# First stage of a layer stack: low rows, projections, slot logits and gate in another order, with the logits' operands filled to 128 partitions

## The chip, the cores and the metric

The kernel runs on one core of one Trainium2 chip. The metric is the time on the device of one execution, in microseconds (us); less is better. The median of three runs is 1717.63 us (1714.06 to 1718.74).

## The reference

Eight sequences of 512 tokens with 128 features go through eight residual layers, each on the layer-normed stream. The change touches only the first layer, a slot attention with 4 heads of 32 features and 64 slots per head. Cut to what matters:

```python
q, k = rope(x @ Wq), rope(x @ Wk); v = x @ Wv
sk = clip(x @ sk_w1 @ sk_w2 + sk_b2, -32, 32)      # sk_w1: 128 -> 16, sk_w2: 16 -> 256
sv = clip(x @ sv_w1 @ sv_w2 + sv_b2, -32, 32)
wk = exp(sk); zk = cumsum(wk, over tokens)
S = where(mask, q @ k.T, 0)
p = softmax((S @ wk) * scale / zk)                  # over the 64 slots
wv = exp(sv); zv = cumsum(wv, over tokens)
A = where(mask, (p / zv) @ wv.T, 0)
o = rms_norm(A @ v) * gnorm_w
g = x @ Wg
x = x + (o * g * sigmoid(g)) @ Wo
```

All of it is in float32. The seven later layers are not touched.

## The kernel before, in words

The work of the first layer lies in `slot_phase` (L2457), with the operations in the class `SlotAttention` (L1828) and the layer norm in `Norm` (L182). It is a software pipeline written out by hand: the program of each engine is a list in which step `s` works on several sequences at once. `batch(s, lag)` gives the sequence `s - lag` if there is one. Lag 0 is the new sequence (norm, projections, rope), lag 1 the middle one (slot weights, scores, logits), lag 2 the last one (softmax, attention, output), lag 3 the output projection and the residual. There are eight sequences and eleven steps; steps 2 to 7 carry all three main lags. The order on every engine is fixed, and one engine waits for another only through semaphores. PSUM has eight banks; the plan in `Banks` (L92) says in which order the products of a step take each bank, and TensorE (PE) waits before it writes a bank until its earlier reader is through.

The operations that the prediction walks through, with the engine of each:

- `rope` (L1958 to L1964, POOL): four products and two sums for queries and keys of one sequence, once all four `qkv_copy` are done. `sum_two`, `Norm.scale`, `sum_three` follow it in POOL's list.
- `states`, `turn_k`, `turn_q`, `scores` (PE): they need the turned queries and keys. `k_copy` (L2089) and `q_copy` (L2096, ACT) bring the transposed keys and queries to SBUF.
- `Norm.normalise` (L262, ACT), then `Norm.turn` (L269, PE) and `Norm.copy` (L275, ACT) for the new sequence.
- `value_log` (L2065) and `value_inverse` (L2070, ACT): one over the running sums of lag 2. `over_sums` (L2204, DVE) needs them; behind it in DVE's list stand `mask_scores` (L2130), and behind those wait `attend` (L2216, PE) and `slot_logits` (L2144, L2150).
- `low` (L1907, PE) makes 32 low rows from the normed sequence, `low_copy` (L1913, ACT) puts them into the tile `lowT`, whose row 33 is ones; `slot` (L1969, PE) multiplies these 33 rows with `slot_w2` for one quarter of the tokens, `clip` (L1979, DVE) and `weights` (L1983, ACT) finish the slot weights.
- `gate` (L1928, PE), `gate_guard` and the three steps of `gate_sigmoid` (L1935 to L1944, ACT), `gate_product` (L1948, DVE).
- `project` (L1918, PE) and `qkv_copy` (L1923, ACT), four times a sequence; `mean_squares` (L2251), `project_out` (L2275), `inverse_rms` (L2256, L2258), `apply_rms` (L2263), `apply_gate` (L2269), `add` (L2281); `scan` (L2058, DVE), the running sums.

PE's step before ends with `project` 3 and 2, `low`, `gate`, `slot` 1 and 0, and the next begins with `slot` 2 and 3 and `key_sums` 0. ACT's step begins with the rest of the last projection, `low_copy`, the whole gate chain and `weights` 1 and 0. After this phase the stages of the later layers follow one another, each with its own programs.

Of the kernel before, what the change touches and what calls it, by code (L numbers as in the profile page):

```python
# [14 lines left out]
P = 128  # L15
NB = 8
T = 512
# [1810 lines left out]
class SlotAttention:  # L1828
# [5 lines left out]
    def __init__(self, nc, sv, tag, norm, last_slot):  # L1834
# [11 lines left out]
        self.last_slot = last_slot  # L1846
        self.lowT = sb("lowT", [2 * LOW + 1, T])
        self.qkv = sb("qkv", [P, NT, 3 * D], 3)
# [40 lines left out]
    def set_up_rows(self, dve):  # L1889
        for u in range(2):  # L1890
            last = dve.memset(self.lowT[u][2 * LOW:2 * LOW + 1, :], 1.0)
        last.then_inc(self.ones_row, 1)
# [16 lines left out]
    def low_copy(self, act, b):  # L1909
        act.wait_ge(self.low_done, b + 1)  # L1910
        act.wait_ge(self.ones_row, 1)
        wait_ge(act, self.slot_done[self.last_slot], b - 1)
        act.activation(self.lowT[b % 2][0:2 * LOW, :], self.banks.of("low")[0:2 * LOW, :], ACT.Copy).then_inc(self.lowT_ready, 1)  # L1913
# [22 lines left out]

    def gate_sigmoid(self, act, b):
        sig = self.sig[b % 2]
        act.wait_ge(self.g_steps, 3 * b + 1)
        act.activation(sig[:, :], sig[:, :], ACT.Exp, scale=-1.0, bias=self.consts[:, 1:2]).then_inc(self.g_steps, 1)  # L1940
        act.wait_ge(self.g_steps, 3 * b + 2)
        act.activation(sig[:, :], sig[:, :], ACT.Ln, bias=self.sv.ones[:, 0:1]).then_inc(self.g_steps, 1)
        act.wait_ge(self.g_steps, 3 * b + 3)
        act.activation(sig[:, :], sig[:, :], ACT.Exp, scale=-1.0).then_inc(self.sig_ready, 1)  # L1944
# [512 lines left out]
def slot_phase(nc, sv, tag, a):  # L2457
# [3 lines left out]
    with nc.cleanup_on_exit():  # L2461
# [5 lines left out]
        banks = Banks(nc, tag, 8, (  # L2467
            ("slot2", 2, 1, (slot.clip_done[2],)), ("slot3", 3, 1, (slot.clip_done[3],)), ("zk0", 5, 1, (slot.zk_ready[0],)),
            ("state1", 7, 1, (slot.state_ready[1],)), ("kT", 5, 1, (slot.kT_ready,)), ("qT", 6, 1, (slot.qT_ready,)),
# [4 lines left out]
            ("A0", 0, 2, (slot.a_ready[0],)), ("A1", 1, 2, (slot.a_ready[1],)), ("A2", 2, 2, (slot.a_ready[2],)), ("A3", 3, 2, (slot.a_ready[3],)),  # L2474
            ("L1", 6, 1, (slot.lg_ready[1],)), ("L0", 5, 1, (slot.lg_ready[0],)), ("proj1", 1, 0, (slot.qkv_ready[1],)),
            ("o", 4, 2, (slot.on_ready,)), ("proj0", 0, 0, (slot.qkv_ready[0],)), ("wvT1", 6, 1, (slot.wvT_ready[1],)),
            ("ms", 5, 2, (slot.ln_ready,)), ("out", 6, 3, (slot.x_done,)), ("proj3", 3, 0, (slot.qkv_ready[3],)), ("proj2", 2, 0, (slot.qkv_ready[2],)),
            ("low", 4, 0, (slot.lowT_ready,)), ("gT", 5, 0, (slot.gated_ready,)), ("slot1", 1, 0, (slot.clip_done[1],)), ("slot0", 0, 0, (slot.clip_done[0],))))
        norm.banks = slot.banks = banks
# [14 lines left out]
        with nc.Block() as block:  # L2494
# [16 lines left out]
            def _(pe):  # L2511
                pe.wait_ge(constants, ALL_CONSTANTS)
                pe.wait_ge(memsets, 3)
                for s in STEPS:
                    for b in batch(s, 1):
                        slot.slot(pe, b, 2)
                        slot.slot(pe, b, 3)
                        slot.key_sums(pe, b, 0)
                        slot.states(pe, b, 1)
                        slot.turn_k(pe, b)  # L2520
                        slot.turn_q(pe, b)
                        slot.states(pe, b, 2)
                        slot.scores(pe, b)
# [18 lines left out]
                    for b in batch(s, 1):  # L2542
                        slot.slot_logits(pe, b, 1)
                        slot.slot_logits(pe, b, 0)
                    for b in batch(s, 0):
# [5 lines left out]
                    for b in batch(s, 1):  # L2551
                        slot.turn_values(pe, b, 1)
                    if s == LAST:
                        pe.wait_ge(folding.products_kept, 1)
# [7 lines left out]
                    for b in batch(s, 0):  # L2562
                        slot.project(pe, b, 3)
                        slot.project(pe, b, 2)
                        slot.low(pe, b)
                        slot.gate(pe, b)
                        slot.slot(pe, b, 1)
                        slot.slot(pe, b, 0)
                folding.turn_ternary(pe, 0)

            @block.scalar
            def _(act):
# [4 lines left out]
                for s in STEPS:  # L2577
                    for b in batch(s, 1):
                        slot.qkv_copy(act, b, 2)
                        slot.low_copy(act, b)  # L2580
                        slot.gate_guard(act, b)
                        slot.gate_sigmoid(act, b)
                        slot.weights(act, b, 1)
                        slot.weights(act, b, 0)
                    for b in batch(s, 2):
                        slot.exponential(act, b)
                    if s == LAST:
                        folding.copy(act)
                    for b in batch(s, 1):
                        slot.weights(act, b, 2)  # L2590
                        slot.key_log(act, b, 0)
                    for b in batch(s, 2):
                        slot.value_log(act, b)
                    for b in batch(s, 1):
                        slot.k_copy(act, b)
                        slot.q_copy(act, b)
                    for b in batch(s, 0):
                        norm.normalise(act, b)
                    for b in batch(s, 1):
                        slot.weights(act, b, 3)  # L2600
                    for b in batch(s, 2):
                        slot.value_inverse(act, b)
                    for b in batch(s, 1):
                        slot.key_log(act, b, 1)
                        slot.values_copy(act, b, 0)
                        slot.key_inverse(act, b)
                    for b in batch(s, 0):
                        norm.copy(act, b)
                    if s == LAST:
                        folding.keep_products(act)  # L2610
                    for b in batch(s, 2):
                        slot.square(act, b)
                    for b in batch(s, 0):
                        slot.qkv_copy(act, b, 1)
                    for b in batch(s, 1):
                        slot.values_copy(act, b, 1)
                    for b in batch(s, 2):
                        slot.inverse_rms(act, b)
                    for b in batch(s, 0):
                        slot.qkv_copy(act, b, 3)  # L2620
                        slot.qkv_copy(act, b, 0)
                folding.finish_proj(act)

            @block.vector
            def _(dve):
                slot.set_up_rows(dve)
                for s in STEPS:
                    for b in batch(s, 0):
                        norm.statistics(dve, b)
                        norm.aggregate(dve, b)  # L2630
                    if s == 0:
                        dve.wait_ge(constants, ALL_CONSTANTS)
                        dve.wait_ge(memsets, 3)
                    for b in batch(s, 1):
                        slot.clip(dve, b, 1)
                        slot.clip(dve, b, 0)
                        slot.gate_product(dve, b)
                        slot.clip(dve, b, 2)
                    for b in batch(s, 2):
                        slot.scan(dve, b, 1)  # L2640
                    for b in batch(s, 1):
                        slot.clip(dve, b, 3)
                        slot.state_copy(dve, b, 1)
# [3 lines left out]
                    for b in batch(s, 1):  # L2647
                        slot.state_copy(dve, b, 2)
                        slot.mask_scores(dve, b, 0)
                    for b in batch(s, 2):  # L2650
# [24 lines left out]
                    for b in batch(s, 1):  # L2675
                        slot.scale_logits(dve, b, 0)
                        slot.maximum(dve, b)
                        slot.subtract(dve, b)
                        slot.scan(dve, b, 0)
                    for b in batch(s, 2):  # L2680
                        slot.apply_rms(dve, b)
                    if s != LAST:
                        for b in batch(s, 3):
                            slot.add(dve, b)
                    for b in batch(s, 2):
                        slot.apply_gate(dve, b)
                folding.finish_fc(dve)
# [318 lines left out]
def program(nc, a, out):  # L3006
# [35 lines left out]
    sv.slot_w1 = sb("slot_w1", [P, 2 * LOW], F32)  # L3042
    sv.slot_w2 = sb("slot_w2", [2 * LOW + 1, 2 * SH * SM], F32)
    sv.l1b_w = sb("l1b_w", [P, 6, D], F32)
# [31 lines left out]
```

## Time and profile before

| | before |
|---|---|
| median of three runs | 1717.63 us |
| time of the profiled execution | 1717.68 us |
| its span (first to last instruction) | 1715.9 us |
| PE busy | 1520.5 us, 89% of the span |
| DVE busy | 1189.5 us, 69% |
| ACT busy | 1256.8 us, 73% |
| POOL busy | 529.5 us, 31% |
| mean granted TensorE clock | 0.940 of full speed |

A timeline row gives the start in us from the span's start, the time it took, the engine, the line, the operation and its tiles, how many instructions are merged in it, and in brackets how long the engine was idle before it and who ended that. Busy time of PE is modelled at its ends, so the distance from one start to the next is the safer measure.

### The profile page before, as it was taken

The page shows a single profiled execution, that of the slowest core. Times are in us where ns is not written, and L with a number is a line of the kernel's source. Part 1 is how long each engine was busy: PE and PEld are TensorE (multiplying, and loading weights), DVE is VectorE, ACT ScalarE, POOL GpSimd, SP SyncE. Part 2 cuts the span into 40 slices and gives each one's busy share as a digit, 9 for nine tenths or more (in the row PEclk, how much of TensorE's full clock was granted, in tenths as well). Part 3 has the DMA queues.
Part 4 walks back from the last instruction along what each step waited for, and adds up shares of the span by engine and source line. Part 5 has one row for each costly group of instructions (what it writes and reads, how often), then busy time and mean ns, then how long its engine had stood idle before and what let it go on. Part 6 is the DMA issues. An engine that isn't in the chain of part 4 may idle for free. (4 is left out here: it accounts for less than half of the span.)

```text
span 1715.9 us, 37883 instructions
## 1 busy us (share of the span) xinstructions
PE 1520.5 (89%) x14142; PEld 731.0 (43%) x14142; DVE 1189.5 (69%) x1931; ACT 1256.8 (73%) x2113; POOL 529.5 (31%) x908
## 2 busy tenths in 40 slices
PE   7899997784699999998889999968874999999998
PEld 4676665662133333336633333345541333333256
DVE  4677778798999999966710000048878999999743
ACT  4555553597488888885679999925763888888863
POOL 3432342552323333334400000013212233333362
PEclk9899989797699999999989999989986999999999
DMA  4000000025534343320133333201333333333211
GB/s 132 1 1 1 1 1 1 1 78 156 155 97 110 108 112 107 109 64 27 38 94 95 96 100 97 68 24 49 99 106 113 84 90 92 87 93 93 67 38 38
DMA packets 140410, 125.42 MB, mean 73 GB/s; under 512 B 38410, under 2 KB 118340, under 8 KB 140228
## 3 DMA queue, kind: packets, MB, share of 16 engines
q1 hardware_dynamic: 130980, 121.90, 23.9%
q0 software_dynamic: 8192, 0.77, 0.9%
q8 instruction: 113, 1.85, 0.5%
q14 instruction: 69, 0.57, 0.1%
q10 hardware_dynamic: 1056, 0.33, 0.1%
HBM read 77.19 MB, written 44.96 MB: 71 GB/s over the span
## 5 line engine op out<-in xcount | busy, mean ns | idle before, releaser
L1700 ACT ACTIVATE m_probs<-m_psum 128x512 f32<-128x512 f32 (+1 forms) x768 | 511.7, 762 | 63.1 <-PE m_psum L1623 62.2
L1700 ACT ACTIVATE e_probs<-e_psum 128x512 f32<-128x512 f32 x512 | 276.3, 596 | 53.3 <-PE e_psum L1623 51.8
L1740 DVE TENSOR_REDUCE a_minus_max<-m_psum 128x2 f32<-128x1024 f32 x256 | 300.9, 1219 | 14.3 <-PE m_psum L1632 13.0
L1740 DVE TENSOR_REDUCE a_minus_max<-e_psum 128x2 f32<-128x1024 f32 x256 | 300.6, 1219 | 14.4 <-PE e_psum L1632 13.0
L1623 PE MATMUL m_psum<-m_q_stack,m_k_stack 114*32 114x512 bf16 (+1 forms) x4096 | 295.8, 385 | 6.7 <-DMA m_k_stack<-n_parts 4.6
L1643 PE MATMUL m_psum<-m_probs,m_v_ones 128*32 128x512 f32 x2048 | 271.0, 602 | 3.4 <-DVE m_pair L1690 2.1
L1623 PEld LDWEIGHTS m_psum<-m_q_stack,m_k_stack 114*32 114x32 bf16 (+1 forms) x4096 | 106.9, 96 | 225.8 <-issue 126.2
L1623 PE MATMUL e_psum<-e_q_stack,e_k_stack 126*32 126x512 bf16 x2048 | 157.8, 385 | 2.2 <-ACT e_probs L1700 2.2
L1643 PE MATMUL e_psum<-e_probs,e_v_ones 128*32 128x512 f32 x1024 | 132.2, 593 | 0.0
L1632 PE MATMUL m_psum<-m_k_stack,m_q_stack 48*128 48x512 bf16 x512 | 93.0, 400 | 32.0 <-DVE a_minus_max L1740 24.4
L1632 PE MATMUL e_psum<-e_k_stack,e_q_stack 60*128 60x512 bf16 x512 | 93.9, 400 | 27.9 <-DVE a_minus_max L1740 22.6
L1583 POOL CAST a_max_parts<-a_minus_max 128x16 bf16<-128x16 f32 x64 | 12.6, 197 | 324.6 <-DVE a_minus_max L1740 324.6
L1522 POOL DMA_DIRECT2D m_q_stack<-a_max_rows x128 | 76.3, 602 | 58.6 <-DVE a_max_rows L1745 51.4
L1522 POOL DMA_DIRECT2D e_q_stack<-a_max_rows x128 | 76.2, 601 | 58.0 <-DVE a_max_rows L1745 51.0
L1623 PEld LDWEIGHTS e_psum<-e_q_stack,e_k_stack 126*32 126x32 bf16 x2048 | 43.7, 95 | 116.9 <-ACT e_probs L1700 70.5
L1958 POOL TENSOR_TENSOR s_rope_product<-s_qkv,rope 128x512 f32<-128x512 f32 x32 | 40.3, 1291 | 156.0 <-ACT s_qkv L1923 156.0
L1577 POOL COPY m_v_ones<-vtok 128x128 f32<-128x128 f32 x64 | 18.5, 289 | 222.1 <-PE m_psum L1643 222.1
L1643 PEld LDWEIGHTS m_psum<-m_probs,m_v_ones 128*32 128x32 f32 x2048 | 53.0, 110 | 78.5 <-ACT m_probs L1700 51.9
L1690 DVE COPY slot_w<-m_psum 128x512 f32<-128x512 f32 x8 | 5.5, 691 | 113.4 <-PE m_psum L1643 113.4
L1632 PEld LDWEIGHTS m_psum<-m_k_stack,m_q_stack 48*128 48x128 bf16 x512 | 24.6, 93 | 114.6 <-issue 53.7
L1632 PEld LDWEIGHTS e_psum<-e_k_stack,e_q_stack 60*128 60x128 bf16 x512 | 24.6, 93 | 113.2 <-issue 53.8
L1413 DVE RECIPROCAL slot_wo<-slot_wo 128x64 f32<-128x64 f32 x24 | 13.1, 546 | 80.3 <-DMA slot_wo<-a_context_pairs 80.3
(401 smaller groups left out, 2648.1 us busy)
## 6 DMA issues: line engine op xcount, KB each, us to landing
polar_q<-m_late SPq DMA_DIRECT2D x24, 256.0 KB, 3.0
polar_k<-m_late SPq DMA_DIRECT2D x24, 256.0 KB, 3.4
m_q_stack<-polar_q SPq DMA_DIRECT2D x64, 96.0 KB, 2.3
m_k_stack<-polar_k SPq DMA_DIRECT2D x64, 96.0 KB, 2.4
ctx<-a_context_pairs SPq DMA_DIRECT2D x48, 128.0 KB
a_context_pairs<-slot_w SPq DMA_DIRECT2D x24, 256.0 KB, 2.2
m_q_stack<-dist_parts SPq DMA_DIRECT2D x192, 32.0 KB
m_k_stack<-dist_parts SPq DMA_DIRECT2D x192, 32.0 KB
```

The lines of the kernel that those rows point to most:

```text
L1413: dve.reciprocal(self.inverse, self.sums).then_inc(self.inverted, 1)
L1522: pool.dma_start(rows[:, :, j:j + 32], self.max_rows[j:j + 32, :]).then_inc(self.rows_loaded, 16)
L1577: pool.tensor_copy(self.buf.v_ones[n % 2][:, :, :, DH * (n % 2):DH * (n % 2) + DH], self.sv.vtok[:, tiles_of(b), :].rearrange("p t (h d) - ...
L1583: pool.tensor_copy(self.max_parts[:, 0, :], self.minus_max[n % 2][:, :]).then_inc(self.hi_ready, 1)
L1623: last = pe.matmul(self.ps_s[i % self.PAIRS][r:r + 32, j, :], self.buf.k_stack[g][0:self.rows, h, c * P + r:c * P + r + 32], self.buf.q_st ...
L1632: pe.matmul(to[:, :], self.buf.q_stack[g][part, h, t * P:(t + 1) * P], self.buf.k_stack[g][part, h, :], start=True, stop=True).then_inc(se ...
L1643: last = pe.matmul(self.ps_pv[32 * h:32 * h + self.buf.VW, :], self.buf.v_ones[m % 2][:, c, h, :], self.buf.probs[(NT * m + c) % self.buf. ...
L1690: copied = eng.tensor_copy(self.buf.pair[k % 2][:, :], self.ps_pv[:, :])
L1700: act.activation(self.buf.probs[(NT * m + c) % self.buf.PROBS][:, self.WIDE * part:self.WIDE * (part + 1), :], self.ps_s[i % self.PAIRS], ...
L1740: dve.tensor_reduce(self.minus_max[n % 2][:, k:k + NT + 1:NT], self.ps_r[r % self.TWOS], AX.X, ALU.max, negate=True).then_inc(self.two_fre ...
L1958: pool.tensor_tensor(self.products[n][:, :, :, :], halves[:, :, :, i, :], table, ALU.mult).then_inc(self.rope_steps, 1)
```

## The change

`lowT` and `slot_w2` grow from 33 to 128 partitions. The rows beyond 33 are zeros on both sides, so the products stay the same: `slot_w2` is cleared whole as before, and each `lowT` is cleared once at the start. `gate_sigmoid` is split into three calls, so that ACT's list can put other work between them. The orders of the lists are changed: on PE `low` goes between the two halves of `slot_logits`, `project` 3 and 2 ahead of `mean_squares`, `gate` behind `slot` 1 and 0, and `key_sums` 0 between `slot` 2 and `slot` 3. `gT` moves from bank 5 to bank 4. On ACT `weights` 1 and 0 close a step, and the gate chain comes after `key_log` 0, laced with `k_copy`, `q_copy` and `weights` 3; `value_log` and `normalise` come behind it. On DVE the statistics of the next sequence move ahead of `scan` 0, `clip` 1 and 0 and `scan` 1 move to the end of the step, and `gate_product` moves behind `state_copy` 2. POOL's list stays.

```diff
-        self.lowT = sb("lowT", [2 * LOW + 1, T])
+        self.lowT = sb("lowT", [P, T])
...
     def set_up_rows(self, dve):
         for u in range(2):
+            last = dve.memset(self.lowT[u][:, :], 0.0)
+        last.then_inc(self.ones_row, 1)
+        dve.wait_ge(self.ones_row, 1)
+        for u in range(2):
             last = dve.memset(self.lowT[u][2 * LOW:2 * LOW + 1, :], 1.0)
...
-            ("slot2", 2, 1, ...), ("slot3", 3, 1, ...), ("zk0", 5, 1, ...),
+            ("slot2", 2, 1, ...), ("zk0", 5, 1, ...), ("slot3", 3, 1, ...),
...
-            ("low", 4, 0, (slot.lowT_ready,)), ("gT", 5, 0, (slot.gated_ready,)), ("slot1", 1, 0, ...), ("slot0", 0, 0, ...)))
+            ("slot1", 1, 0, ...), ("slot0", 0, 0, ...), ("gT", 4, 0, (slot.gated_ready,))))
...
 PE
                         slot.slot(pe, b, 2)
+                        slot.key_sums(pe, b, 0)
                         slot.slot(pe, b, 3)
-                        slot.key_sums(pe, b, 0)
...
                         slot.slot_logits(pe, b, 1)
+                    for b in batch(s, 0):
+                        slot.low(pe, b)
+                    for b in batch(s, 1):
                         slot.slot_logits(pe, b, 0)
...
                         slot.turn_values(pe, b, 1)
+                    for b in batch(s, 0):
+                        slot.project(pe, b, 3)
+                        slot.project(pe, b, 2)
...
                     for b in batch(s, 0):
-                        slot.project(pe, b, 3)
-                        slot.project(pe, b, 2)
-                        slot.low(pe, b)
-                        slot.gate(pe, b)
                         slot.slot(pe, b, 1)
                         slot.slot(pe, b, 0)
+                        slot.gate(pe, b)
 ACT
                     for b in batch(s, 1):
-                        slot.qkv_copy(act, b, 2)
-                        slot.low_copy(act, b)
-                        slot.gate_guard(act, b)
-                        slot.gate_sigmoid(act, b)
-                        slot.weights(act, b, 1)
-                        slot.weights(act, b, 0)
+                        slot.weights(act, b, 2)
                     for b in batch(s, 2):
                         slot.exponential(act, b)
...
                     for b in batch(s, 1):
-                        slot.weights(act, b, 2)
                         slot.key_log(act, b, 0)
+                        slot.gate_guard(act, b)
+                        slot.k_copy(act, b)
+                        slot.gate_exponential(act, b)
+                        slot.q_copy(act, b)
+                        slot.gate_logarithm(act, b)
+                        slot.weights(act, b, 3)
+                        slot.gate_sigmoid(act, b)
                     for b in batch(s, 2):
                         slot.value_log(act, b)
-                    for b in batch(s, 1):
-                        slot.k_copy(act, b)
-                        slot.q_copy(act, b)
                     for b in batch(s, 0):
                         norm.normalise(act, b)
-                    for b in batch(s, 1):
-                        slot.weights(act, b, 3)
                     for b in batch(s, 2):
                         slot.value_inverse(act, b)
...
                         norm.copy(act, b)
+                        slot.low_copy(act, b)
...
+                        slot.qkv_copy(act, b, 3)
+                        slot.qkv_copy(act, b, 2)
                     for b in batch(s, 2):
                         slot.inverse_rms(act, b)
                     for b in batch(s, 0):
-                        slot.qkv_copy(act, b, 3)
-                        slot.qkv_copy(act, b, 0)
+                        slot.weights(act, b, 1)
+                        slot.weights(act, b, 0)
 DVE
                     for b in batch(s, 1):
-                        slot.clip(dve, b, 1)
-                        slot.clip(dve, b, 0)
-                        slot.gate_product(dve, b)
                         slot.clip(dve, b, 2)
-                    for b in batch(s, 2):
-                        slot.scan(dve, b, 1)
...
                         slot.state_copy(dve, b, 2)
+                        slot.gate_product(dve, b)
                         slot.mask_scores(dve, b, 0)
...
+                    for b in batch(s + 1, 0):
+                        norm.statistics(dve, b)
+                        norm.aggregate(dve, b)
                         slot.scan(dve, b, 0)
                     for b in batch(s, 2):
                         slot.apply_rms(dve, b)
+                    for b in batch(s, 0):
+                        slot.clip(dve, b, 1)
+                        slot.clip(dve, b, 0)
+                    for b in batch(s, 2):
+                        slot.apply_gate(dve, b)
                         ... slot.add(dve, b)
-                        slot.apply_gate(dve, b)
+                    for b in batch(s, 1):
+                        slot.scan(dve, b, 1)
...
-    sv.slot_w2 = sb("slot_w2", [2 * LOW + 1, 2 * SH * SM], F32)
+    sv.slot_w2 = sb("slot_w2", [P, 2 * SH * SM], F32)
```

## Rows read from the trace of the kernel before

**Rows 1.** Timeline of PE: one step at 177 to 211 us, and the first step.

```profile
27.79 0.70 PE L269 MATMUL s_bank<-ident,s_n_xn 128*128 128x128 f32 x4
...
177.88 1.04 PE L1907 MATMUL s_bank<-s_n_xnT,slot_w 128*32 128x512 f32 x2
...
179.91 3.70 PE L1969 MATMUL s_bank<-slot_w,s_lowT 33*128 33x512 f32 x8
...
187.39 0.70 PE L2103 MATMUL s_bank<-vtok,s_qk 128*128 128x256 f32 x2 [0.50 <-POOL s_qk L1964]
...
197.08 2.06 PE L2216 MATMUL s_bank<-s_zvT,s_wvT 64*128 64x128 f32 x32 [0.65 <-DVE ctx L2130]
...
208.14 1.02 PE L2251 MATMUL s_bank<-s_o,s_same_head 128*128 128x512 f32 x2
...
210.05 1.46 PE L1918 MATMUL s_bank<-slot_w,s_n_xnT 128*128 128x384 f32 x4
211.44 1.04 PE L1907 MATMUL s_bank<-s_n_xnT,slot_w 128*32 128x512 f32 x2
```

**Rows 2.** Timeline of POOL: rope's pieces in four of its eight runs.

```profile
21.83 1.26 POOL L1964 TENSOR_TENSOR s_qk<-s_rope_product 128x512 f32<-128x512 f32 x1
...
48.90 1.27 POOL L1964 TENSOR_TENSOR s_qk<-s_rope_product 128x512 f32<-128x512 f32 x1
...
178.83 5.01 POOL L1958 TENSOR_TENSOR s_rope_product<-s_qkv,rope 128x512 f32<-128x512 f32 x4 [21.77 <-ACT s_qkv L1923]
...
185.15 2.19 POOL L1964 TENSOR_TENSOR s_qk<-s_rope_product 128x512 f32<-128x512 f32 x1
...
253.78 2.18 POOL L1964 TENSOR_TENSOR s_qk<-s_rope_product 128x512 f32<-128x512 f32 x1
```

**Rows 3.** Timeline of ACT in the same step.

```profile
180.74 0.72 ACT L1940 ACTIVATE s_sig<-s_sig,s_consts 128x512 f32<-128x512 f32 x1
...
183.82 1.04 ACT L2178 ACTIVATE s_logits<-s_logits 128x1024 f32<-128x1024 f32 x1
...
188.96 0.60 ACT L2089 ACTIVATE s_kT<-s_bank 128x512 f32<-128x512 f32 x1
189.46 0.59 ACT L2096 ACTIVATE s_qT<-s_bank 128x512 f32<-128x512 f32 x1
189.97 1.65 ACT L262 ACTIVATE s_n_xn<-x,s_n_shift,s_n_rstd 128x128 f32<-128x128 f32 x4
191.52 0.61 ACT L1983 ACTIVATE vtok<-vtok 128x512 f32<-128x512 f32 x1
192.04 1.04 ACT L2070 ACTIVATE s_zvT<-s_zvT 128x1024 f32<-128x1024 f32 x1
```

**Rows 4.** Timeline of DVE in the same step, and one row of step 8.

```profile
175.82 1.23 DVE L2058 TENSOR_TENSOR_SCAN s_zvT<-ones,s_wvT 128x512 f32<-128x512 f32 x1 [1.44 <-ACT s_wvT L2051]
...
178.24 0.68 DVE L2269 TENSOR_TENSOR s_og<-s_og,s_sig 128x512 f32<-128x512 f32 x1
...
184.12 2.16 DVE L2058 TENSOR_TENSOR_SCAN s_zvT<-ones,s_wvT 128x512 f32<-128x512 f32 x1
...
193.19 0.69 DVE L2204 TENSOR_TENSOR s_zvT<-s_bank,s_zvT 128x512 f32<-128x512 f32 x1 [0.37 <-ACT s_zvT L2070]
...
261.36 0.68 DVE L2204 TENSOR_TENSOR s_zvT<-s_bank,s_zvT 128x512 f32<-128x512 f32 x1
```

**Rows 5.** Windows: stretch, length, busy PE, PEld, DVE, ACT, POOL, clock, DMA.

```profile
184.00:186.00 2.00, 2.00 (x5) 1.64 (x6) 2.00 (x2) 1.39 (x2) 2.00 (x2) 0.50 0.00 0
...
214.00:216.00 2.00, 2.00 (x6) 0.94 (x5) 1.21 (x2) 1.90 (x4) 2.00 (x2) 1.00 0.00 0
...
218.00:220.00 2.00, 2.00 (x6) 1.04 (x4) 2.00 (x2) 0.94 (x2) 2.00 (x2) 0.51 0.01 4
```

**Rows 6.** Timeline of DVE at the start of the span.

```profile
0.89 1.02 DVE L1891 MEMSET s_lowT<- 1x512 f32 x2 [0.89 <-PEq L3065]
...
4.14 0.87 DVE L213 BATCH_NORM_STATS2 s_n_stats<-x 128x6 f32<-128x128 f32 x4 [2.22 <-DMA x<-n_L_attn_a_hidden_states]
```

More of the change, by code:

```diff
@@ L1910, in low_copy @@
         act.wait_ge(self.low_done, b + 1)
-        act.wait_ge(self.ones_row, 1)
+        act.wait_ge(self.ones_row, 2)
         wait_ge(act, self.slot_done[self.last_slot], b - 1)
@@ L1935, in gate_guard, with gate_exponential @@
         act.activation(sig[:, :], self.banks.of("gT")[:, :], ACT.Relu, bias=self.consts[:, 1:2]).then_inc(self.g_steps, 1)
-    def gate_sigmoid(self, act, b):
+    def gate_exponential(self, act, b):
         sig = self.sig[b % 2]
@@ L1940, in gate_sigmoid, with gate_logarithm @@
         act.activation(sig[:, :], sig[:, :], ACT.Exp, scale=-1.0, bias=self.consts[:, 1:2]).then_inc(self.g_steps, 1)
+    def gate_logarithm(self, act, b):
+        sig = self.sig[b % 2]
         act.wait_ge(self.g_steps, 3 * b + 2)
         act.activation(sig[:, :], sig[:, :], ACT.Ln, bias=self.sv.ones[:, 0:1]).then_inc(self.g_steps, 1)
+    def gate_sigmoid(self, act, b):
+        sig = self.sig[b % 2]
         act.wait_ge(self.g_steps, 3 * b + 3)
@@ L2467, in slot_phase @@
         banks = Banks(nc, tag, 8, (
-            ("slot2", 2, 1, (slot.clip_done[2],)), ("slot3", 3, 1, (slot.clip_done[3],)), ("zk0", 5, 1, (slot.zk_ready[0],)),
+            ("slot2", 2, 1, (slot.clip_done[2],)), ("zk0", 5, 1, (slot.zk_ready[0],)), ("slot3", 3, 1, (slot.clip_done[3],)),
             ("state1", 7, 1, (slot.state_ready[1],)), ("kT", 5, 1, (slot.kT_ready,)), ("qT", 6, 1, (slot.qT_ready,)),
@@ L2474, in slot_phase @@
             ("A0", 0, 2, (slot.a_ready[0],)), ("A1", 1, 2, (slot.a_ready[1],)), ("A2", 2, 2, (slot.a_ready[2],)), ("A3", 3, 2, (slot.a_ready[3],)),
-            ("L1", 6, 1, (slot.lg_ready[1],)), ("L0", 5, 1, (slot.lg_ready[0],)), ("proj1", 1, 0, (slot.qkv_ready[1],)),
+            ("L1", 6, 1, (slot.lg_ready[1],)), ("low", 4, 0, (slot.lowT_ready,)), ("L0", 5, 1, (slot.lg_ready[0],)), ("proj1", 1, 0, (slot.qkv_ready[1],)),
             ("o", 4, 2, (slot.on_ready,)), ("proj0", 0, 0, (slot.qkv_ready[0],)), ("wvT1", 6, 1, (slot.wvT_ready[1],)),
-            ("ms", 5, 2, (slot.ln_ready,)), ("out", 6, 3, (slot.x_done,)), ("proj3", 3, 0, (slot.qkv_ready[3],)), ("proj2", 2, 0, (slot.qkv_ready[2],)),
-            ("low", 4, 0, (slot.lowT_ready,)), ("gT", 5, 0, (slot.gated_ready,)), ("slot1", 1, 0, (slot.clip_done[1],)), ("slot0", 0, 0, (slot.clip_done[0],))))
+            ("proj3", 3, 0, (slot.qkv_ready[3],)), ("proj2", 2, 0, (slot.qkv_ready[2],)), ("ms", 5, 2, (slot.ln_ready,)), ("out", 6, 3, (slot.x_done,)),
+            ("slot1", 1, 0, (slot.clip_done[1],)), ("slot0", 0, 0, (slot.clip_done[0],)), ("gT", 4, 0, (slot.gated_ready,))))
         norm.banks = slot.banks = banks
@@ L2608, in _ @@
                         norm.copy(act, b)
+                        slot.low_copy(act, b)
                     if s == LAST:
                         folding.keep_products(act)
+                    for b in batch(s, 0):
+                        slot.qkv_copy(act, b, 1)
                     for b in batch(s, 2):
@@ L2613, in _ @@
                     for b in batch(s, 0):
-                        slot.qkv_copy(act, b, 1)
+                        slot.qkv_copy(act, b, 0)
                     for b in batch(s, 1):
                         slot.values_copy(act, b, 1)
+                    for b in batch(s, 0):
+                        slot.qkv_copy(act, b, 3)
+                        slot.qkv_copy(act, b, 2)
                     for b in batch(s, 2):
@@ L2626, in _ @@
                 slot.set_up_rows(dve)
+                norm.statistics(dve, 0)
+                norm.aggregate(dve, 0)
+                dve.wait_ge(constants, ALL_CONSTANTS)
+                dve.wait_ge(memsets, 3)
                 for s in STEPS:
[L2628 to L2633, printed above, removed]
                     for b in batch(s, 1):
-                        slot.clip(dve, b, 1)
-                        slot.clip(dve, b, 0)
-                        slot.gate_product(dve, b)
                         slot.clip(dve, b, 2)
-                    for b in batch(s, 2):
-                        slot.scan(dve, b, 1)
-                    for b in batch(s, 1):
                         slot.clip(dve, b, 3)
@@ L2681, in _ @@
                         slot.apply_rms(dve, b)
+                    for b in batch(s, 0):
+                        slot.clip(dve, b, 1)
+                        slot.clip(dve, b, 0)
+                    for b in batch(s, 2):
+                        slot.apply_gate(dve, b)
                     if s != LAST:
@@ L2684, in _ @@
                             slot.add(dve, b)
-                    for b in batch(s, 2):
-                        slot.apply_gate(dve, b)
+                    for b in batch(s, 1):
+                        slot.scan(dve, b, 1)
                 folding.finish_fc(dve)
```

## The prediction

> **What bounds the first stage now.** The page's first part shows PE as the busiest engine, 89% of the span, so at first sight PE bounds it. The timelines of the four engines, read side by side for one step, say otherwise for this stage. Follow one turn of the pipeline. P is the moment at which PE has issued the last `project` (177.88, where `low` begins [rows 1]). The copies and rope's start follow by 178.83, and rope ends at R = 187.34 [rows 2]: P to R is 9.46 us. PE waits for it (0.50 us [rows 1]), turns the keys, and ACT's `k_copy` starts at 188.96, R + 1.62 [rows 3]. ACT goes on to `q_copy`, `normalise`, `weights` 3 and `value_inverse`, and DVE's `over_sums` starts at 193.19, which is 4.23 after `k_copy` [rows 4]. Four more pieces of DVE's list lie ahead of `attend` at 197.08 (3.89 us; PE waits 0.65 [rows 1]). From there PE works without a long wait to the next P at 211.44: 14.36 us [rows 1]. The five legs, 9.46 + 1.62 + 4.23 + 3.89 + 14.36, make 33.56 us, the distance from one P to the next. So the step is a ring of dependences through POOL, ACT, DVE and PE, and an operation is free if it lies beside this ring and paid for in every step if it lies on it.
>
> From the second rope's end (50.17) to the eighth's (255.96) six turns take 205.79 us, 34.30 each [rows 2]. That is 4.4 us more than six times 33.56.
>
> **The clock.** The windows of 2 us show it. In 214 to 216 us PE is busy all 2.00 us, with the 33-row products, at a granted clock of 1.00; in 218 to 220 it is as busy and the clock is 0.51. In the step before, it is 0.50 in 184 to 186 [rows 5], just behind the run of eight 33-row products that begins at 179.91 [rows 1]. Every step has such a fall behind this run. Where it is short it lies inside the wait for rope and the step keeps its 33.56 us; where it is long it reaches past R, and the step takes about 1.5 us more: three of six, by the 4.4 us above.
>
> **The change, part by part.**
>
> *The zero rows.* A product over 33 rows and one over 128 stream the same 512 columns; two of them take 2.03 us together as `low` and `gate` (177.88 to 179.91), four slots 3.70 [rows 1]: no cost, at most 0.1 us a slot. If the clock then stays up, the gain is what the fall costs now, 0 to 1.5 us a step, 4.4 us in all, and no more, because in the other steps rope is waited for anyway. I take it as gained: the full-clock step is my base. The two memsets more (two small ones take 1.02 [rows 6]) fit in the 2.22 us in which DVE waits for the first input; without that cover they would cost about 1 us once.
>
> *PE from `attend` to P.* `low` comes in (half of 2.03, 1.0 us). `mean_squares` and `project_out` go behind P (210.05 - 208.14 = 1.91 us [rows 1]). The leg becomes 14.36 + 1.0 - 1.91 = 13.45. `low` needs `Norm.copy`, which ACT has done long before; `outputs` needs `low_copy` because of bank 4, hidden behind the second `slot_logits` and a projection. Gain 0.91.
>
> *PE from P to R.* It now has `mean_squares`, `project_out`, `slot` 1 and 0, `gate`, `slot` 2, `key_sums` 0 and `slot` 3, some 7.6 us against 9.46: PE waits nearly 2 us for rope instead of 0.5. That costs nothing itself; the ring passes through POOL here. `gate`'s new wait, for `apply_rms` to free bank 4, is met while `slot` 1 and 0 run.
>
> *ACT between `k_copy` and `over_sums`.* This is the costly part. Now four operations stand there. After the change they are, in ACT's order: `k_copy`, the gate's first step, `q_copy`, its second, `weights` 3, its third, `value_log`, `normalise`, `value_inverse`. None from the gate's first step on can start before `k_copy`, which waits for rope. A copy of 0.60 lets the next start after 0.50 (188.96 to 189.46), so I take 0.1 off each duration: 0.50 + 0.62 + 0.50 + 0.62 + 0.52 + 0.52 + 0.94 (as the 1.04 of the 1024-wide exponential) + 1.55 (189.97 to 191.52) + 1.15 (192.04 to `over_sums` at 193.19) [rows 3, 4]. That is 6.92 against 4.23: 2.69 us more. What is late next: `normalise` starts 4.22 us after `k_copy` instead of 1.01 (188.96 to 189.97), so `Norm.turn` on PE, and all that is queued behind it (`states` 3, `key_sums` 1, `turn_values`, `attend`), waits. `gate_product`, which must free bank 4 for `Norm.turn`, is ready before the normed rows are and hides behind them. `over_sums` blocks DVE's list, with three `mask_scores` behind it, so `attend` moves by the full 2.69.
>
> *Port and queue in P to `k_copy`.* `scan` 1 runs beside rope now: it takes 2.16 instead of 1.23, and rope's last piece 2.19 instead of 1.26 [rows 2, 4]. After the change it still does. New beside rope is `apply_gate` (0.68 [rows 4]), which reads two SBUF operands as the scan does. Bounds for what rope loses: 0 and 0.68; by the scan's row, where 0.93 of 1.23 was lost, 0.5, which I take. `clip` 2, `weights` 2, `exponential` and `key_log` 0 queue behind the later `scan` 1 and come through about when rope ends; `k_copy` is 0 to 0.6 late by them, I take 0. The statistics move into time in which DVE waited.
>
> New turn: 9.46 + 0.5 + 1.62 + 6.92 + 3.89 + 13.45 = 35.84, against 34.30 as measured: 1.54 more, six times, 9.2 us.
>
> *The ends.* At the start `low` precedes the projections: rope 0 is 1.0 us later. In step 1, without lag 2, `Norm.turn` began 4.70 after R (27.79 against 23.09 [rows 1, 2]); ACT now starts `normalise` at 1.62 + 3.28 = 4.90 and has all four pieces at 6.5, so `Norm.turn` ends some 1.5 later; less the 0.91, 0.6. In step 8, without lag 0, `over_sums` came at R + 5.40 (261.36 [rows 4] after 255.96 [rows 2]); now 1.62 + 3.28 + 0.94 + 1.15 = 6.99: 1.6. The last two steps keep their chain.
>
> Sum: 9.2 + 1.0 + 0.6 + 1.6 = 12.4 us. The profiled execution took 1717.68 us, as the median (1717.63): **1730 us**. Bounds: with no loss of rope and 0.1 us less for each of seven ACT operations the turn is 34.6 and the sum 5 us; with both losses at their upper ends 36.6 and 17 us: 1723 to 1735.
>
> **The rivals.**
>
> *The clock falls all the same, in the new waits.* For it: PE now waits about 2 us for rope, then again for the normed rows and `over_sums`; against it: the rows above show the fall behind 33-row products on a busy PE. If it falls where the turn goes through PE behind R, it costs the 1.5 us of the long falls now, eight times: 12 us on top, 1742. This is also the case in which zeros do nothing. The Trainium skill (TensorE: Matmul & The Clock Gate, section "Why this matters for your kernels") puts a fall down to idle gaps between bursts of matmuls, and by it zero rows would help nothing while longer waits would hurt; this trace disagrees so far, since PE was busy 2.00 of 2.00 us ahead of the fall.
>
> *Faster: ACT's longer list hides.* It decides at `over_sums`: if that starts under R + 6.8 (5.85 now and the 0.91 gained behind `attend`), the step gets shorter. If ACT had the gate's steps and `value_log` done ahead of R, where it idles, the turn would be 33.56 - 0.91 = 32.65: six times 1.65 gained, 0.9 in step 1, 1.0 lost at the start, 1708. For it: ACT has idle time enough, and the clock's gain comes with it. Against: in the program's order they stand behind `k_copy`, which can't precede rope.
>
> *About even.* If the operations overlap better than I take (34.3 a turn) and only the ends lose, 1720.
>
> **How the numbers follow.** A measurement of this kernel can tell about 0.3%, 5 us, from no change. My forecast 0.53, the falling clock 0.15, about even 0.15, faster 0.17. So slower 0.68, same 0.15, faster 0.17. The likeliest case's own range is 1723 to 1735. The range of 8 in 10 reaches from 1710 into the falling clock at 1744; left out is most of the faster case.
>
> **What would show it.** In the profile after: rope's ends about 35.8 us apart; PE waiting about 2 us for rope at L2103 and 1 to 2 us at L269 for ACT's normed rows; `over_sums` at R + 8.5; the clock at 1.00 behind the slots. Wrong it is if `over_sums` comes before R + 7, if rope starts more than 1 us behind P, or if the clock's falls grow longer than now.

## The result

The changed kernel takes 1735.98 us in the median (1734.28 to 1738.26, four runs) against 1718.14: 1.0107 of before (95% interval 1.0092 to 1.0122), so slower by 1.1%, clear of the noise. The profiled execution took 1735.14 us, with a span of 1733.3; before it was 1717.68 and 1715.9, so the profiles differ by 17.4 us.

The first stage carries nearly all of it. The first row of the next stage on PE, of before and then of after (timelines):

```profile
311.20 1.63 PE L269 MATMUL m_psum<-ident,m_probs 128*128 128x128 f32 x4 [6.42 <-ACT m_probs L262]
```

```profile
327.97 1.63 PE L269 MATMUL m_psum<-ident,m_probs 128*128 128x128 f32 x4 [6.42 <-ACT m_probs L262]
```

That is 16.8 of the 17.4 us. (Line numbers after: rope L1968 to L1974, `states` L2113, `k_copy` L2099, `value_log` L2075, `value_inverse` L2080, `over_sums` L2214, `slot` L1979, `weights` L1993, the gate's ACT lines L1939 to L1954.) One step of after, read as [rows 1 to 4] were, PE first:

```profile
188.54 1.02 PE L2261 MATMUL s_bank<-s_o,s_same_head 128*128 128x512 f32 x2
...
198.33 0.70 PE L2113 MATMUL s_bank<-vtok,s_qk 128*128 128x256 f32 x2 [2.29 <-POOL s_qk L1974]
...
204.78 1.39 PE L269 MATMUL s_bank<-ident,s_n_xn 128*128 128x128 f32 x4 [0.82 <-ACT s_n_xn L262]
...
207.68 1.19 PE L2018 MATMUL s_bank<-vtok,causal 128*128 128x256 f32 x2 [0.67 <-DVE s_zvT L2214]
...
211.66 2.06 PE L2226 MATMUL s_bank<-s_zvT,s_wvT 64*128 64x128 f32 x32
...
224.77 1.02 PE L2261 MATMUL s_bank<-s_o,s_same_head 128*128 128x512 f32 x2
```

ACT and DVE of the same step:

```profile
199.97 0.60 ACT L2099 ACTIVATE s_kT<-s_bank 128x512 f32<-128x512 f32 x1 [0.23 <-PE s_bank L2086]
200.46 0.71 ACT L1944 ACTIVATE s_sig<-s_sig,s_consts 128x512 f32<-128x512 f32 x1
...
202.16 0.63 ACT L1993 ACTIVATE vtok<-vtok 128x512 f32<-128x512 f32 x1
202.68 0.62 ACT L1954 ACTIVATE s_sig<-s_sig 128x512 f32<-128x512 f32 x1
203.20 1.05 ACT L2075 ACTIVATE s_zvT<-s_zvT 128x1024 f32<-128x1024 f32 x1
204.15 1.64 ACT L262 ACTIVATE s_n_xn<-x,s_n_shift,s_n_rstd 128x128 f32<-128x128 f32 x4
205.69 1.04 ACT L2080 ACTIVATE s_zvT<-s_zvT 128x1024 f32<-128x1024 f32 x1
```

```profile
192.82 0.95 DVE L2279 TENSOR_TENSOR s_og<-s_og,s_sig 128x512 f32<-128x512 f32 x1
...
206.84 0.69 DVE L2214 TENSOR_TENSOR s_zvT<-s_bank,s_zvT 128x512 f32<-128x512 f32 x1 [2.21 <-ACT s_zvT L2080]
```

POOL: rope's end in the second run, rope in this step, its start in the next, and the end of the eighth:

```profile
54.65 1.26 POOL L1974 TENSOR_TENSOR s_qk<-s_rope_product 128x512 f32<-128x512 f32 x1
...
189.46 5.45 POOL L1968 TENSOR_TENSOR s_rope_product<-s_qkv,rope 128x512 f32<-128x512 f32 x4 [23.73 <-ACT s_qkv L1927]
...
197.02 1.26 POOL L1974 TENSOR_TENSOR s_qk<-s_rope_product 128x512 f32<-128x512 f32 x1
...
225.69 5.45 POOL L1968 TENSOR_TENSOR s_rope_product<-s_qkv,rope 128x512 f32<-128x512 f32 x4 [24.14 <-ACT s_qkv L1927]
...
269.44 1.27 POOL L1974 TENSOR_TENSOR s_qk<-s_rope_product 128x512 f32<-128x512 f32 x1
```

With P and R as in the prediction (the last `project` issued, rope's end), P is 188.54 and R is 198.28: 9.74 us (it was 9.46 [rows 1, 2]). `k_copy` follows at R + 1.69, and `over_sums` 6.87 after that (it was 4.23 [rows 3, 4]), with DVE idle for 2.21 us until ACT's `value_inverse`. PE waits at the three places that the forecast named: 2.29 for rope, 0.82 for the normed rows (1 to 2 was forecast), 0.67 for `over_sums`. From `over_sums` to `attend` this step takes 4.82 instead of the 3.89 of before: PE's granted clock falls there (0.50, the last figure but two of the window), while the other five turns keep 3.80 to 3.89.

```profile
209.00:211.00 2.00, 2.00 (x6) 1.55 (x5) 1.38 (x3) 0.00 (x0) 0.00 (x0) 0.50 0.00 0
```

Six turns, from 55.91 to 270.71, take 35.80 us each; before, 34.30 [rows 2].

Below, a *turn* is this figure for each kernel, from its one profile: end of the eighth rope less end of the second, over six. Each ratio is to the kernel before on the same chip.

### The profile page after: what moved, and what is told of

Its sections match the earlier page's. It is cut to its first block and busy times, and to the rows that moved or that the text cites. A ratio compares the mean times of both kernels' runs of the same rounds, so it can differ in the third digit from the quotient of the medians.

```text
span 1733.3 us, 37886 instructions
## 1 busy us (share of the span) xinstructions
PE 1516.9 (88%) x14142; PEld 732.3 (42%) x14142; DVE 1190.9 (69%) x1933; ACT 1257.1 (73%) x2113; POOL 532.6 (31%) x908
## 5 line engine op out<-in xcount | busy, mean ns | idle before, releaser
L1968 POOL TENSOR_TENSOR s_rope_product<-s_qkv,rope 128x512 f32<-128x512 f32 x32 | 44.5, 1422 | 168.1 <-ACT s_qkv L1927 168.1
```

The lines of the kernel that those rows point to most:

```text
L1968: pool.tensor_tensor(self.products[n][:, :, :, :], halves[:, :, :, i, :], table, ALU.mult).then_inc(self.rope_steps, 1)
```

## The experiments

| kernel | turn, us | ratio to before (95%) |
|---|---|---|
| before | 34.30 | 1 |
| changed | 35.80; 36.21 again | 1.0107; 1.0111 (1.0091 to 1.0131) again |
| old order, zero rows | 33.83 | 0.9976 (0.9966 to 0.9986) |
| new order, 33 rows | 36.48; 36.40 again | 1.0107 (1.0091 to 1.0124); 1.0122 (1.0102 to 1.0142) again |
| changed, gate chain ahead | 33.78 | 1.0009 (0.9998 to 1.0019) |
| and value_log ahead, weights 3 and gate_product moved | 32.57 | 0.9961 (0.9949 to 0.9974) |
| that, and low behind in step 0 | 32.76 | 0.9947 (0.9932 to 0.9963) |
| the same, 33 rows | 32.82 | 0.9954 (0.9941 to 0.9966) |
| the same, 128 rows, PE filled | 32.12 | 0.9941 (0.9926 to 0.9956) |
| changed, PE filled | 35.25 | 1.0076 (1.0060 to 1.0091) |
| old order, zeros, projections ahead | 33.86 | 0.9975 (0.9962 to 0.9987) |

**Zero rows without the order, and the order without zero rows.** The first adds the two tile sizes and the memsets of the diff to the kernel before:

```diff
-        self.lowT = sb("lowT", [2 * LOW + 1, T])
+        self.lowT = sb("lowT", [P, T])
```

> The order of before with the zero rows alone (logits' operands over 128 partitions). Theory (the step is a ring through rope, ACT, DVE and PE; the clock falls behind the 33-row products, and zero rows hold it): no fall behind the slots, all six full turns near 33.6 us instead of 33.6 and 35.1, so about 4.4 us less than before, 1713 to 1715. Rival (falls come from idle gaps of PE alone, zeros do nothing): falls at the same places, turns of 33.6 and 35.1 as before, 1718 within 2 us.

Measured: 0.9976, the size that was expected. Over 45 to 245 us the mean granted clock (the last figure but two) is 0.92 before and 0.98 here:

```profile
45.00:245.00 200.00, 185.32 (x1394) 135.00 (x1393) 149.54 (x227) 110.08 (x191) 65.41 (x70) 0.92 0.01 1
```

```profile
45.00:245.00 200.00, 177.45 (x1402) 130.67 (x1401) 151.49 (x229) 112.26 (x195) 65.84 (x71) 0.98 0.00 1
```

So the zero rows hold the clock up, though not in every step as expected: two of the six turns still take 34.87 and 34.47. Where the 4 us are saved this profile does not show. It is of the slowest of the twelve executions (1719.40 us); its turns are 2.8 us shorter in sum, but it reaches the next stage at 311.32, no sooner than before (311.20). The second has the new order and the 33 rows back:

> The new order with 33 rows as before. Theory: the order is the whole loss, since k_copy to over_sums stays 6.87 us; without zeros the clock falls in every step, by 0 to 1.5 us a turn on top of 35.2 at full clock: 1736 to 1745. Rival (zeros do nothing for the clock in the new order): 1736 within 3 us, with the same number of falls as in the changed kernel (six of 3.4 us in steps 0 to 7).

1.0107 at first, so it was run again beside the changed kernel:

> The changed kernel once more, beside its twin with 33 rows on the same chip. Both theories: 1.0107 of before, within 0.0015.

> The new order with 33 rows, beside the changed kernel on the same chip. Theory (zero rows hold the clock in this order too; turns of 36.5 against 35.8 us, 4.4 us of the first stage in the profiles): 3 to 5 us slower than the changed kernel. Rival (what the first stage gains, later stages lose by their own clock falls, so that nothing is left in the whole time): within 1.5 us of the changed kernel.

1.0111 and 1.0122: the intervals overlap widely. The medians differ by 2.4 us, between the 1.5 of the rival and the 3 to 5 of the theory, and the turns by 0.7 us in the first pair of profiles (35.80, 36.48) and 0.2 in the second (36.21, 36.40). In the new order a gain of the zeros can't be told from the noise. With 33 rows or 128 the loss is there: it is the order's.

**ACT's list.** First the gate chain alone goes ahead, into time in which ACT waits for `clip` 2:

```diff
                     for b in batch(s, 1):
+                        slot.gate_guard(act, b)
+                        slot.gate_exponential(act, b)
+                        slot.gate_logarithm(act, b)
+                        slot.gate_sigmoid(act, b)
                         slot.weights(act, b, 2)
...
                         slot.k_copy(act, b)
                         slot.q_copy(act, b)
                         slot.weights(act, b, 3)
```

> The changed kernel, with ACT's gate chain (guard and three steps) moved ahead of weights 2, where ACT waits for clip 2; value_log stays behind q_copy. Theory: the three gate steps lie on the ring, so k_copy to over_sums falls from 6.87 to about 5.1 us and a turn from 35.8 to about 34.0; with step 1 and step 8 about 14 us less: 1722. Rival (ACT's list is hidden and the loss comes from rope's start, the port shared by DVE and POOL, or PE): k_copy to over_sums gets shorter but the turn does not, 1736 within 3 us.

Then `value_log` too. This edit makes two more moves: `weights` 3 goes behind `value_inverse`, and `gate_product` goes ahead of `state_copy` 1, nearer to its old place:

> As the kernel with the gate chain ahead, and value_log ahead of k_copy, weights 3 behind value_inverse, gate_product on DVE behind clip 3. Theory: normalise is then bound by POOL's scale (about 2.6 us behind rope's end), over_sums about 5.4 us behind rope's end; the shorter way from attend to rope remains as a gain, so a turn of about 32.6 to 33.0 us, 1709 to 1714, below before. Rival (another wait takes its place at once, k_copy late behind value_log or the scan beside rope): a turn of 33.5 to 34.3, 1718 to 1723.

ACT in one step of the second kernel (timeline):

```profile
180.65 0.69 ACT L1939 ACTIVATE s_sig<-s_bank,s_consts 128x512 f32<-128x512 f32 x1 [0.34 <-DVE s_og L2279]
...
185.83 1.05 ACT L2075 ACTIVATE s_zvT<-s_zvT 128x1024 f32<-128x1024 f32 x1
187.07 0.60 ACT L2099 ACTIVATE s_kT<-s_bank 128x512 f32<-128x512 f32 x1 [0.19 <-PE s_bank L2086]
187.93 0.60 ACT L2106 ACTIVATE s_qT<-s_bank 128x512 f32<-128x512 f32 x1 [0.26 <-PE s_bank L2093]
188.42 1.64 ACT L262 ACTIVATE s_n_xn<-x,s_n_shift,s_n_rstd 128x128 f32<-128x128 f32 x4
189.96 1.05 ACT L2080 ACTIVATE s_zvT<-s_zvT 128x1024 f32<-128x1024 f32 x1
```

The gate's steps and `value_log` are through before `k_copy`, and only three operations are left between it and `over_sums`. The turn falls by 2.02 us with the gate chain (1.8 was expected) and by 1.21 more with the second edit, 3.23 of 35.80. From `k_copy` to `over_sums` it is 5.12 us with the gate chain ahead and 3.68 with the second edit, in the steps without a fall of the clock. `weights` 3 has a part in the last 1.44: in the changed kernel `value_log` takes 0.95 from start to start, `weights` 3 0.52. No run takes the two apart. The theory's numbers are met in both but for 0.03 us of a turn (32.57, where 32.6 to 33.0 was expected), and the second kernel is below before. `attend` to rope's start stays at 14.03 us in both, against 15.30 before, so that part of the new order is a gain.

**PE's idle time.** Two needless products go behind `slot` 3, where PE waits for rope; the output is untouched:

```diff
                         slot.slot(pe, b, 3)
+                        slot.fill(pe, b, 2)
                         slot.states(pe, b, 1)
```

> The changed kernel with two needless products of 128 rows by 512 columns (1.7 us, into a bank that is free then) on PE behind slot 3, where it waits 2.3 us for rope. Theory (in the new order the falls come from PE's idle time ahead of rope's end, and each costs the ring about 0.9 us): almost no falls in steps 1 to 7, rope's end to k_copy 1.7 us in each, turns of 35.2 instead of 35.8 to 36.2, 3 to 6 us less than the changed kernel, 1.008 of before. Rival (the falls follow the sparse stretch behind rope's end, whatever comes ahead): as many falls, 1.011.

The changed kernel before this edit, around one end of rope (windows), and then both over 45 to 245 us, the filled one last:

```profile
161.00:163.00 2.00, 0.50 (x2) 0.47 (x3) 0.33 (x1) 2.00 (x4) 2.00 (x3) 1.00 0.00 0
163.00:165.00 2.00, 2.00 (x12) 1.97 (x12) 1.18 (x2) 1.22 (x3) 1.76 (x6) 0.56 0.00 0
```

```profile
45.00:245.00 200.00, 171.85 (x1262) 125.32 (x1261) 143.03 (x223) 108.03 (x187) 71.22 (x72) 0.96 0.00 1
```

```profile
45.00:245.00 200.00, 177.48 (x1325) 125.95 (x1323) 144.11 (x224) 109.90 (x189) 71.33 (x72) 1.00 0.01 1
```

PE stands idle for 1.5 of 2 us and the clock then falls. With the wait filled it stays at 1.00 in all of the steps, the turn is 35.25 and each is within 0.15 of the others. More work on PE made the kernel faster: 1.0076, where the changed kernel had 1.0107 and 1.0111. The 35.25 is the order at full clock; the 34.30 of before has falls in it.

**The start, and the best version.** In step 0 alone `low` goes behind the projections, and `low_copy` on ACT likewise; all else is as in the kernel with `value_log` ahead:

```diff
                         slot.project(pe, b, 3)
                         slot.project(pe, b, 2)
+                        if s == 0:
+                            slot.low(pe, b)
```

> The kernel with gate chain and value_log ahead, with low and low_copy behind the projections in step 0 alone. Theory: low ahead of the projections costs 1.8 us at the half clock of the start, so rope 0 starts about 1.8 us earlier (15.7 to 15.9) and the whole is 1.8 us shorter than without this edit. Rival (the start is hidden, since PE waits 2.8 us for rope 0 and ACT's list sets step 1): less than 0.5 us.

Rope 0 starts at 16.04 instead of 17.58, 1.5 us earlier (1.8 was expected). The ratio moves from 0.9961 to 0.9947, in the direction and about the size, but the intervals overlap.

> The fastest kernel so far (gate chain and value_log ahead, low behind the projections in step 0) with 33 rows instead of 128. Theory (zero rows are worth little where the falls come from idle time ahead of rope's end): at most 2 us slower, 0.995 to 0.997 of before. Rival (they hold the clock here as in the old order): 3 to 5 us slower, 0.997 to 0.998.

0.9954, as the theory had it: no difference from 128 rows that can be told.

> The fastest kernel so far with the same two needless products. Theory: falls in steps 1 to 7 go, turns of 32.1 us instead of 32.8, about 4 us less, 0.992 to 0.993 of before. Rival: as many falls, 0.995.

0.9941, 1706.83 us in the median, with turns of 32.12 as expected. It is the lowest of all and below both kernels. In whole time the expectation of 0.992 to 0.993 was missed, and the kernel can't be told from the same without filling. ACT and DVE of one of its steps:

```profile
182.01 0.59 ACT L2104 ACTIVATE s_kT<-s_bank 128x512 f32<-128x512 f32 x1
...
185.69 0.68 DVE L2219 TENSOR_TENSOR s_zvT<-s_bank,s_zvT 128x512 f32<-128x512 f32 x1
```

The two filled kernels show the price of ACT's list with no fall of the clock in any step: from `k_copy` to `over_sums` 3.68 here instead of 6.87, 3.19 us, and the turn 32.12 instead of 35.25, 3.13 us.

**One move of PE, in the old order.** `project` 3 and 2 go ahead of `mean_squares`, with zero rows; `gate` goes ahead of `low`, and in ACT's list (not printed here) `gate_guard` goes ahead of `low_copy`:

```diff
                         slot.turn_values(pe, b, 1)
+                        slot.project(pe, b, 3)
+                        slot.project(pe, b, 2)
...
                     for b in batch(s, 0):
-                        slot.project(pe, b, 3)
-                        slot.project(pe, b, 2)
-                        slot.low(pe, b)
                         slot.gate(pe, b)
+                        slot.low(pe, b)
```

> The order of before with zero rows and one move of the change alone: projections 3 and 2 ahead of mean_squares and project_out (gate ahead of low, ACT's copies in the order of the projections). Theory: attend to rope's start shrinks by 1.91 us, from 15.3 to 13.4; k_copy to over_sums stays 4.2; low, now waiting for apply_rms in bank 4, makes key_sums 0 end some 0.7 us behind rope: a turn of about 32.4 us, 1706 to 1710. Rival (PE's own list behind P, with low, gate and four slots, then sets the turn): rope's end to k_copy grows by 2 us or more, a turn of 33.5, 1714 to 1717.

0.9975, as with zero rows alone: a miss, and about the rival's numbers. `attend` to rope's start did shrink, to 13.3, but from the third rope on `k_copy` came 3.3 to 6.2 us behind rope's end instead of 1.6. `low_copy` sat in ACT's list behind `gate_guard`, which waits for `apply_gate`, and the slots came late. PE and ACT of one step:

```profile
178.98 1.02 PE L1911 MATMUL s_bank<-s_n_xnT,slot_w 128*32 128x512 f32 x2 [0.29 <-DVE s_og L2267]
182.26 3.70 PE L1973 MATMUL s_bank<-slot_w,s_lowT 128*128 128x512 f32 x8 [2.26 <-ACT s_lowT L1917]
```

```profile
181.05 0.69 ACT L1939 ACTIVATE s_sig<-s_bank,s_consts 128x512 f32<-128x512 f32 x1 [2.94 <-DVE s_og L2273]
181.64 0.57 ACT L1917 ACTIVATE s_lowT<-s_bank 32x512 f32<-32x512 f32 x1
```

In the change `low` and `low_copy` come earlier and have no such wait; that this is what lets its shorter way count is argued from these rows, not shown by a run.

## Why the prediction was right, and where its terms were off

1730 was forecast and 1736 measured: inside the range, 1 us above the likeliest case's own 1723 to 1735, slower as forecast, by the mechanism named as likeliest. Step by step:

- **ACT between `k_copy` and `over_sums`**: 6.92 forecast, 6.87 measured in all six turns. With the gate chain, `value_log` and `weights` 3 moved out of this stretch it is 3.68, and the turn is 3.13 us shorter at full clock. This is shown, not argued; only how the second edit's share splits between `value_log` and `weights` 3 is not.
- **The turn**: 35.84 forecast, 35.80 and 36.21 measured, but that it is so close is luck in part, since errors cancel. At full clock it is 35.25 (the filled kernel). Rope lost 0.28 beside DVE, where I took 0.5 (`apply_gate` itself took 0.95 instead of 0.68 [rows 4]). `attend` to rope's start is 14.03 in every turn, where I had 13.45 and 0.95, 14.40; a wait of 0.30 us on PE ahead of `outputs` went, which I had left in. Against these 0.6 stand 0.55 to 0.96 of clock falls, which I had put into a rival and not into the sum.
- **The falling clock** (rival): half right. It does fall in the new waits, but costs about 0.6 to 1 us a turn, not 1.5. The Trainium skill's rule on idle gaps (TensorE: Matmul & The Clock Gate, section "Why this matters for your kernels") names idle gaps between matmuls as the cause. It fits the new order in kind, where filling a wait took the mean clock from 0.96 to 1.00, though the gap that it warns of is longer than this wait of 2.29 us; it does not cover the old one, where 128 rows in place of 33 on a busy PE took it from 0.92 to 0.98.
- **The zero rows**: 4.4 us forecast as what the falls cost in the old order; 0.24%, 4.1 us, measured there, of which the profile shows 2.8 in the turns. In the new order the forecast's base, a full clock in every step, did not hold: the clock falls six times between the first rope's end and the eighth's, and no gain can be told. The two memsets cost nothing, as forecast: PE's first product of the first sequence starts at 8.84 us in both profiles.
- **The start**: 1.0 us forecast, 2.4 measured (rope 0 ends at 25.51 instead of 23.09). I took `low` at the 1.0 us of the later steps. Here it holds PE from 10.47 to 12.29, 1.8 us, and the projections behind it take 0.6 longer. Such a duration fits the lower clock, but the windows show 1.00 from 10 to 12 us, so the reason is not shown. The size varies too: in the six other profiles with `low` in this place, rope 0 starts 1.0 to 2.1 us later than before (2.5 here). After (PE, timeline):

```profile
10.47 1.89 PE L1911 MATMUL s_bank<-s_n_xnT,slot_w 128*32 128x512 f32 x2 [0.78 <-ACT s_n_xnT L275]
12.29 4.91 PE L1922 MATMUL s_bank<-slot_w,s_n_xnT 128*128 128x384 f32 x8
17.03 1.88 PE L1979 MATMUL s_bank<-slot_w,s_lowT 128*128 128x512 f32 x4
```

- **Step 1**: 0.6 us forecast, 3.3 measured (rope's first to second end 30.40 instead of 27.08). The step that failed is "less the 0.91". That gain comes from moving `mean_squares` and `project_out`, which have no sequence yet in step 1, so `low` only adds, 1.0. The delay of `Norm.turn` came out at 1.7 (1.5 forecast), and rope took 0.6 longer (9.39 instead of 8.79), with DVE's two scans beside it.
- **Step 8 and the end**: 1.6 forecast, 2.0 measured from the eighth rope to the next stage.

These make 2.4 + 3.3 + 9.0 + 2.0 = 16.7 of the profiles' 17.4 us; the sum of the forecast was 12.4, and the start and step 1 are what it lacked. The second profile of the same kernel splits otherwise, 1.5 + 4.3 + 11.5 + 2.5 = 19.8, so each part is good to one or two us, not to a tenth.

The faster rival is gone for the reason given: nothing behind `k_copy` in ACT's list can precede rope. Its number, 32.65, is close to the 32.57 of the kernel with the gate and `value_log` ahead, but by luck: that kernel has a shorter stretch from `k_copy` to `over_sums` than the rival assumed (3.68, with `weights` 3 gone, instead of 4.23) and a shorter way from `attend` to rope, while falls of the clock and the longer rope take some of it back.

## What to carry to other kernels

Read several engines' timelines of one step side by side and close the ring of dependences before believing the busiest engine; here PE was 89% busy, and yet a few small ACT operations behind one copy set the step. On an in-order engine, ask of each moved operation which wait stands ahead of it in its new place, and check that what a move takes away exists in the first and last steps too.

## What was not expected of the hardware

Needless work made a kernel faster: 1.7 us of products in each step raised PE's granted clock to 1.00 over the steps (it was 0.96) and took 0.55 us off a turn of 35.80. And stages whose code is untouched shift by some us from one execution to the next: behind the row at which the next stage begins, the changed kernel took 1405.3 us in its first profile and 1410.7 in its second. Likewise the first profile with the new order and 33 rows reached the next stage at 332.39 us, 4.4 later than the changed kernel, but its whole span was only 1.1 us longer (1734.4). The rest was made up in later stages, whose lists are the same.
